# Mask rows in the score stacks, six slots, and scores issued ahead of values, in a windowed-attention block kernel

## What is computed

```python
q = (x @ Wq + bq).reshape(B, S, H, hd).transpose(0, 2, 1, 3)   # k and v alike, H = 16, hd = 8
scores = jnp.einsum('bhqd,bhkd->bhqk', q, k) * scale
allowed = (j <= i) & (i - j < WINDOW)                          # WINDOW = 32
scores = jnp.where(allowed, scores, NEG_INF)
attn = jax.nn.softmax(scores, axis=-1)
out = jnp.einsum('bhqk,bhkd->bhqd', attn, v)
out = out.transpose(0, 2, 1, 3).reshape(B, S, D)
return out @ Wo + bo
```

## Time and profile before

| | us |
|---|---|
| median of 3 runs | 146.55 (146.3 to 146.96) |
| profiled execution | 145.36 |
| its span, first to last instruction | 143.6 |
| TensorE busy | 110.2 (77%) |
| VectorE busy | 96.1 (67%) |
| ACT busy | 68.9 (48%) |
| GpSimd busy | 46.2 (32%) |
| transfer queue q1 | 20.26 MB, 49.4% of 16 engines |

### The profile page before, as it was taken

The page is one execution under the profiler, slowest core; times in us unless marked ns, Lnnn a source line. Parts: engine busy times, 40 slices in busy tenths (PEclk is TensorE's granted clock), DMA queues, the critical chain, the costliest instruction groups (busy, mean ns, idle before and its releaser), DMA issues.

```text
span 143.6 us, 6819 instructions
## 1 busy us (share of the span) xinstructions
PE 110.2 (77%) x2888; PEld 78.5 (55%) x2888; DVE 96.1 (67%) x254; ACT 68.9 (48%) x157; POOL 46.2 (32%) x67
## 2 busy tenths in 40 slices
PE   0368619579846959966868768587699999999992
PEld 0235505357634746844646546475455649595891
DVE  1571508998697979967969979999999551111031
ACT  3125604556466357445738639438724772433300
POOL 3473360739424006006005103602900299200000
PEclk9999986857999996899999999999999999999999
DMA  1699693946697866596655595491000000202022
GB/s 40 172 324 275 183 333 110 302 120 184 158 262 199 242 183 181 142 286 195 202 175 155 167 293 141 109 258 36 0 5 0 5 2 0 79 1 69 4 73 73
DMA packets 39734, 20.60 MB, mean 143 GB/s; under 512 B 1431, under 2 KB 39582, under 8 KB 39710
## 3 DMA queue, kind: packets, MB, share of 16 engines
q1 hardware_dynamic: 39710, 20.26, 49.4%
HBM read 10.82 MB, written 9.44 MB: 141 GB/s over the span
## 4 chain that ended last, share of the span: by engine, by line
PE 37%; DMA 21%; DVE 18%; issue 10%; SPq 5%; ACT 4%; DVEq 1%; POOL 1%; ACTq 0%
DMA KS<-k_scr 14%; PE bank_o L466 6%; DVE probsT L774 5%; PE bank_qk L584 5%; PE bank_s L489 5%; PE bank_v L584 4%; PE bank_o L489 4%; DMA k_scr<-k_parts 3%; SPq L227 3%; DVE negmax L759 3%; DVE centred L766 2%; DMA q_scr<-q_parts 2%; PE bank_s L443 2%; PE bank_w L512 2%; SPq L210 2%
## 5 line engine op out<-in xcount | busy, mean ns | idle before, releaser
L466 PE MATMUL bank_o<-V,probsT 128*32 128x36 f32 x1024 | 24.9, 206 | 13.1 <-DVE probsT L774 12.4
L654 ACT ACTIVATE probs<-centred 128x512 f32<-128x512 f32 x32 | 20.2, 631 | 26.2 <-DVE probsT L774 17.3
L466 PEld LDWEIGHTS bank_o<-V,probsT 128*32 128x32 f32 x1024 | 21.3, 118 | 18.3 <-issue 13.7
L759 DVE TENSOR_REDUCE negmax<-bank_s 128x8 f32<-128x512 f32 x32 | 21.6, 676 | 8.2 <-PE bank_s L443 8.2
L774 DVE STREAM_TRANSPOSE probsT<-probs 128x512 f32<-128x512 f32 x32 | 22.4, 699 | 0.0
L766 DVE TENSOR_TENSOR centred<-bank_s,negmax 128x512 f32<-128x512 f32 x32 | 21.2, 663 | 0.2
L269 POOL TENSOR_TENSOR q_parts<-rest,q_parts 128x256 bf16<-128x256 f32 x8 | 5.4, 672 | 43.2 <-ACT q_parts L601 43.2
L443 PEld LDWEIGHTS bank_s<-KS,QS 64*32 64x32 bf16 x1024 | 10.3, 98 | 13.2 <-issue 13.2
L436 PE MATMUL bank_s<-masks,ident_bf 128*128 128x512 bf16 x31 | 13.1, 423 | 3.9 <-DMA KS<-k_scr 2.4
L443 PE MATMUL bank_s<-KS,QS 64*32 64x64 bf16 x1024 | 14.6, 199 | 1.6 <-issue 1.6
L601 ACT ACTIVATE V<-bank_v 32x256 f32<-32x256 f32 x32 | 11.9, 371 | 0.4
(11 more groups left out here) (98 smaller groups left out, 200.3 us busy)
## 6 DMA issues: line engine op xcount, KB each, us to landing
QS<-q_scr SPq DMA_DIRECT2D x8, 512.0 KB, 4.2
KS<-k_scr SPq DMA_DIRECT2D x7, 576.0 KB, 5.9
q_scr<-q_parts SPq DMA_DIRECT2D x16, 192.0 KB, 3.0
k_scr<-k_parts SPq DMA_DIRECT2D x16, 192.0 KB, 3.1
q_scr<-q_parts SPq DMA_DIRECT2D x8, 128.0 KB, 3.0
k_scr<-k_parts SPq DMA_DIRECT2D x8, 128.0 KB, 2.2
x_sb<-in_L_attn_x_dram SPq DMA_DIRECT2D x1, 768.0 KB, 5.6
out_dram<-y SPq DMA_DIRECT2D x3, 256.0 KB, 2.3
```

The costliest lines, as they stand in the source:

```text
L466: mm = nc.tensor.matmul(o[q * WIN:(q + 1) * WIN, g * VC:(g + 1) * VC], probsT[s % 2][:, i, g, w, :], V[b][:, j + w, g, :], start=(w == 0), ...
L654: nc.scalar.activation(probs[s % 2][:], centred[s % 2][:].rearrange("p a k -> p (a k)"), ACT.Exp, scale=float(HD) ** -0.5).then_inc(probs_ ...
L759: nc.vector.tensor_reduce(negmax[s % 2][:], bank_s[s % 2][:].rearrange("p (a k) -> p a k", k=2 * WIN), AX.X, ALU.max, negate=True).then_in ...
```

## The change

- The mask is no longer a product of its own. A head's stack has 6 slots x 8 = 48 rows in one half of the 128 partitions; the other half holds an identity (in `QS`) and the mask (`bands`, in `KS`). Even and odd heads use opposite halves, so `QS` and `KS` get a further axis of 2. One score product goes over all 128 rows and adds the mask by the identity rows. The identity product of each unit goes.
- Two of the eight combinations of parts go: the high part is written to 3 slots, the middle part to 2, the low part to 1.
- The stacks are read by four transfers of 48 partitions instead of two of 128.
- VectorE fills the constant rows ahead of the loop (`fill_q`, `fill_k`) and once in step 2 (`fill_pad`). SyncE waits for them ahead of the first reads.
- The masks are made before the first variance root on GpSimd and spread first of all on TensorE.
- On TensorE scores of unit s+1 stand first in a step, ahead of values; `turn_x` moves from u = 1 to u = 0 and `project` from u = 2 to u = 1, and ACT's copies with them. On VectorE the transpose of unit s-2 stands first in a step.
- The clearing of `V[0]` and `V[1]` on GpSimd moves behind the low parts of chunks 0 and 1.

The diff, cut to its core:

```diff
-SLOTS = 8
-Q_PARTS = (range(0, 3), range(3, 6), range(6, 8))
-K_PARTS = (range(0, 8, 3), range(1, 8, 3), range(2, 8, 3))
+SLOTS = 6
+ROWS = HD * SLOTS
+Q_PARTS = (range(0, 3), range(3, 5), range(5, 6))
+K_PARTS = (range(1, 6, 2), range(2, 6, 2), range(0, 1))
...
-        QS = two("QS", [P, 2 * NG, CHUNK], BF16)
-        KS = two("KS", [P, 2 * NG, KW], BF16)
+        QS = two("QS", [P, 2, 2 * NG, CHUNK], BF16)
+        KS = two("KS", [P, 2, 2 * NG, KW], BF16)
...
                 if c >= 2:
                     sp.wait_ge(s_ps, UNITS * (c - 1))
+                else:
+                    sp.wait_ge(filled, 2 * c + 1)
                 sp.wait_ge(q_in[b], WRITES * (c // 2 + 1))
-                sp.dma_start(QS[b][:], q_scr[:, :, cols].rearrange("(n r) c t -> (r c) n t", n=2 * NG)
-                             ).then_inc(stacked[b], 16)
+                for odd in range(2):
+                    rows = slice(2 * WIN * odd, 2 * WIN * odd + ROWS)
+                    sp.dma_start(QS[b][rows, odd], q_scr[:, :, cols].rearrange(
+                        "(n e r) c t -> e (r c) n t", n=2 * NG, e=2)[odd]).then_inc(stacked[b], 16)
...
             ln1_rstd(2, TILES, 2 * TILES)
-            for b in range(2):
-                nc.gpsimd.memset(V[b][:, :, :, 0:GH * HD], 0.0).then_inc(v_set, 1)
             low_parts(0, 0)
+            nc.gpsimd.memset(V[0][:, :, :, 0:GH * HD], 0.0).then_inc(v_set, 1)
...
-                    nc.tensor.matmul(dst[:].rearrange("p (a k) -> p a k", k=2 * WIN), ident_bf[:],
-                                     masks[:, 0:1].to_broadcast([P, UB * NG, 2 * WIN]), start=True, stop=False)
...
-                                dst[hh * WIN:(hh + 1) * WIN, (i * NG + g) * 2 * WIN:(i * NG + g + 1) * 2 * WIN],
-                                QS[b][rows, n, j * WIN:(j + 1) * WIN], KS[b][rows, n, j * WIN:(j + 2) * WIN],
-                                start=False, stop=(i == UB - 1 and g == NG - 1))
+                                bank_s[s % 2][hh * WIN:(hh + 1) * WIN, (i * NG + g) * 2 * WIN:(i * NG + g + 1) * 2 * WIN],
+                                QS[b][:, hh % 2, 2 * g + hh // 2, j * WIN:(j + 1) * WIN],
+                                KS[b][:, hh % 2, 2 * g + hh // 2, j * WIN:(j + 2) * WIN], start=True, stop=True)
...
+                if s + 1 < SU:
+                    scores(turn, s + 1)
+                elif s + 1 == SU and not last:
+                    scores(turn + 1, 0)
                 if not (first and s < 3) and s < SU + 3:
                     values(turn if s >= 3 else turn - 1, (s - 3) % SU)
...
+                    if p1 and u == 0:
+                        turn_x(c + 2, b)
                     if p1 and u == 1:
-                        turn_x(c + 2, b)
-                    if p1 and u == 2:
                         project(c + 2, b)
...
+            def fill_q(b):
+
+                for odd in range(2):
+                    f = nc.vector.tensor_copy(QS[b][:, odd].rearrange("p n (m c) -> p (n m) c", c=2 * WIN),
+                                              ident_bf[:, 2 * WIN * (1 - odd):2 * WIN * (2 - odd)].unsqueeze(1).to_broadcast(
+                                                  [P, NG * BLOCKS, 2 * WIN]))
+                f.then_inc(filled, 1)
...
+            def fill_k(b):
+
+                for odd in range(2):
+                    f = nc.vector.tensor_copy(
+                        KS[b][:, odd, :, WIN:].rearrange("p n (m y k) -> p n m y k", y=2, k=WIN)[:, :, :, 1],
+                        bands[:, odd, 0:WIN].unsqueeze(1).unsqueeze(1).to_broadcast([P, 2 * NG, BLOCKS // 2, WIN]))
+                    f = nc.vector.tensor_copy(
+                        KS[b][:, odd, :, WIN:].rearrange("p n (m y k) -> p n m y k", y=2, k=WIN)[:, :, :, 0],
+                        bands[:, odd, WIN:].unsqueeze(1).unsqueeze(1).to_broadcast([P, 2 * NG, BLOCKS // 2, WIN]))
+                if b == 0:
+                    nc.vector.memset(KS[b][2 * WIN:, 0, :, 0:WIN], NEG)
+                    nc.vector.memset(KS[b][0:2 * WIN, 0, :, 0:WIN], 0.0)
+                    nc.vector.memset(KS[b][0:2 * WIN, 1, :, 0:WIN], NEG)
+                    f = nc.vector.memset(KS[b][2 * WIN:, 1, :, 0:WIN], 0.0)
...
+            dve.wait_ge(consts, 2)
+            fill_q(0)
             dve.wait_ge(x_first, 16)
             ln1_var(0, TILES)
...
             ln1_norm(0, 0)
+            dve.wait_ge(masks_set, 1)
+            fill_k(0)
             dve.wait_ge(x_second, 16)
             ln1_var(TILES, 2 * TILES)
...
+            fill_q(1)
+            fill_k(1)
             split_rest(1, 1)
...
+                if not (first and s < 2) and s < SU + 2:
+                    turn_probs(turn if s >= 2 else turn - 1, (s - 2) % SU)
                 if rows:
                     dve.wait_ge(x1_done, tile + 1)
...
-                if not (first and s < 2) and s < SU + 2:
-                    turn_probs(turn if s >= 2 else turn - 1, (s - 2) % SU)
+                if first and s == 2:
+                    fill_pad(0).then_inc(filled, 1)
```

More of the change, by code:

```diff
@@ L169, in block_kernel @@
         N_FIRST, N_W = 7, 6
-        STACKS = 2 * 16
+        STACKS = 4 * 16
         WRITES = PARTS * 16
@@ L299, in _ @@
-            for first in range(2):
-                nc.gpsimd.affine_select(out=tri[:, first], in_=tri[:, first], compare_op=ALU.is_ge, fill=NEG, base=WIN,
-                                        pattern=[[-1, 2 * WIN]], channel_multiplier=1).then_inc(consts, 1)
+            for row in range(2):
+                for own in range(2):
+                    at = tri[:, row, (1 - own) ^ row:6:4]
+                    nc.gpsimd.affine_select(out=at, in_=at, compare_op=ALU.is_ge if own else ALU.is_gt, fill=NEG, base=0,
+                                            pattern=[[0, 2], [-1 if own else 1, WIN]],
+                                            channel_multiplier=1 if own else -1).then_inc(consts, 1)
@@ L413, in project_v, with spread_bands @@
                 mm.then_inc(v_ps, 1)
[L415 removed]
+            def spread_bands():
                 pe.wait_ge(consts, 6)
[L418 to L420 removed]
+                for quad in range(GH):
+                    e = quad % 2
+                    row, first = (0 if e else 1), (2 if quad < 2 else 0)
+                    mm = nc.tensor.matmul(bank_w[quad * WIN:(quad + 1) * WIN, 0:4 * WIN], ident[0:WIN, 0:WIN],
+                                          tri[:, row, first:first + 4].rearrange("p n k -> p (n k)"), start=True, stop=True)
                 mm.then_inc(masks_ps, 1)
```

63 lines of the change are left out of this document (24 added, 39 removed).

## The result

The change makes the kernel slower: 150.41 us median (149.61 to 150.77, 4 runs) where before has 146.75 (146.3 to 147.8, 4 runs) beside it, a ratio of 1.023 with an interval of 1.016 to 1.030. The interval leaves open whether it is over 2%. The forecast was 139.7, its range ended at 145.0. The profiled execution has a span of 148.7 us; by the forecast it was to be 143.6 − 6.8 = 136.8.

What follows compares the result with a forecast made beforehand. VectorE was taken to bound the loop, TensorE the tail. First unit +1.0, loop waits −7.6, `fill_pad(0)` +0.2 and tail −0.4 sum to −6.8 us: 139.7 us against a median of 146.55, range 136.5 to 145.

Steps and rivals of the forecast that it cites:

- Identity product, 128-row scores: TensorE, each unit: dropping the product gains nothing in the loop, 0.5 us before the first unit; scores take 0.35 us.
- `turn_x` and `project` earlier: Loop: high parts ready about a step (2 us) before the residual split, removing VectorE's 6.0 us of waits.
- Slack 0.4 us at full clock: VectorE's residual add in odd steps: 0.4 us slack, 1.3 us charged for half clock and leftovers, 7.6 of 8.9 gained.
- Available are ... 13.4 − 0.5 = 12.9: Loop: 12.9 us available from split to stack landing against 12.5 needed, so 2.5 us of score waits go.
- The stack load, 6.4 us: New reads of 48 partitions: 6.4 us taken, between 5.2 at full rate and 8.2 at half; no gain.
- Rival (c): Stack reads at half rate: 8.2 us per load, chunks wait, first unit 1.8 us later; 144 us, chance 0.12.
- The fills: VectorE before the loop: `fill_q` 1.4 us, `fill_k(0)` 2.8; with the identity saving, first unit +1.0 us.
- Rival (a): Fills slow or blocked: at 1.0 ns per element the first unit is 5 us late; 143.7 us, chance 0.14.
- Rival (b), the clock: TensorE idles more, clock falls to half: +2.5 us per chunk, 149.7 us at four chunks; chance 0.09.
- Rival (d), waits that only move: Loop: `split_rest` waits for something else, half of the 7.6 us stays; 143.5 us, chance 0.08.
- Idle time of TensorE: Loop of the original kernel: TensorE idle 3 to 5 us per turn, so its saved work gains nothing there.
- The tail: TensorE's last stretch: two identity products (0.6 us) fall out, part still waits on `weff_done`; −0.4 us.

Runs made afterwards that it cites:

- turns_first: Original kernel with VectorE's weight transposes moved to the head of its step, nothing else: 144.47 us against 148.25, first series.
- early_project: Original kernel with only the transposes of x, the q and k projection and their copies one step earlier: 147.17 us, ratio 0.986 from 3 of 11 executions.
- early_turns: Original kernel with the projection one step earlier and VectorE's weight transposes first in the step, scores still behind values: 144.66 us, ratio 0.985.
- after_values_first: Changed kernel with scores put back behind values, output product and projection on TensorE: 147.51 us, ratio 1.003 to the original.
- fill_late: Changed kernel with VectorE's fills of stack 1 moved behind the rest of chunk 1 and the variances of tiles 4 to 7: 146.17 us, ratio 0.998 to the original.
- order_only: Original kernel with only the new order (scores first, transposes first, projection a step earlier): 148.63 us, ratio 1.015.
- boundary_late: Changed kernel with stack 1's fills later and scores behind values at chunk starts alone: 145.04 us, ratio 0.983 to the original.
- combo: Changed kernel with stack 1's fills later and scores behind values, output product and projection in every step: 145.72 us, ratio 0.989 to the original.
- slots_only: Original kernel with only six slots and stack reads of 48 partitions, order and identity product kept: 148.42 us, ratio 1.016.
- turns_first_again: Second series of the original kernel with only VectorE's weight transposes first in the step: 144.99 us, ratio 0.988.
- stacks_turns_first: Changed kernel with stack 1's fills later, transposes first on VectorE, projection and scores at their old places: 146.57 us against 147.52, no ratio.

## Why the prediction was wrong, point by point

- **Identity product, 128-row scores.** Held: 32 products in 0.35 us at full clock (at 41.80), and no gain in the loop.
- **`turn_x` and `project` earlier, "so the 6.0 us go".** The wait went, to 0.4 us; the time did not. The step charged the move as if nothing stood behind that wait. turns_first gives 1.2% without it, early_project nothing that is sure, and both together (early_turns) no more than turns_first.
- **"Slack 0.4 us at full clock ... I charge 1.3 us for this and other leftovers, so that 7.6 of 8.9 us are gained."** This is the step that failed. VectorE idles for 10.8 us in the loop, not 1.3, and the terms of −7.6 and +0.2 came out at +2.9 together (87.78 against 84.93). The prediction named the queue ("what is queued behind the scores' wait") and priced only the half clock in it. What the runs show in its place is 6.7 us of waits for the output projection and 2.3 for the values. 8.0 of these 9.0 us follow stalls of TensorE without a semaphore, which had no term in the sum, and 0.5 a wait for a stack. In the turn without stalls the forecast holds and more, 19.04 us for 19.3 to 19.8. Putting the scores back behind values and output projection gives 3.0 us (after_values_first) but takes only 1.5 to 2.5 of the 10.3 missing in the loop; the cause of the rest is tied to the stalls by their place in the traces, no run takes them away.
- **"Available are ... 13.4 − 0.5 = 12.9."** Wrong as well, by 2.1 us. A stack is wanted 2.6 us ahead of the row maximum when output projection and residual are queued behind it, so 10.8 are available. The chain from split to scores measured 89.91 − 79.16 = 10.75 us, better than the 12.5 forecast, and was just in time. This error costs 0.5 us here, 1.9 in fill_late's third turn and 5.2 in order_only.
- **The stack load, 6.4 us.** From the issue of the first Q read to the scores that wait for it, it takes 7.0 us (82.94 to 89.91) and 7.3 (94.50 to 101.84), with the packets at half rate and a quarter fewer bytes; before needs 7.6 (35.83 to 43.41), 7.8 and 6.6. So 6.4 was too low for both kernels by this measure, and "no gain" held. The Trainium skill's figure in the prediction, 7.2, is met in size, but the rise over before that it implied is not there. Rival (c) was right in its rate and wrong in its price and place: no load of the changed kernel that scores waited for took 8.2 us, and the first unit is not late by it (fill_late).
- **The fills.** Their price held: `fill_q` took 1.3 us (forecast 1.4), `fill_k(0)` 2.4 (forecast 2.8; from 5.64 to 8.08). The Trainium skill's figure in the prediction, 693 ns for 2,048 elements, is the price that the sum took (0.3 × 2,048 + 70 = 684 ns), so it was not near the lower bound, and the "+0.3" worked out from it should have been the sum's own +1.0. What they block was not asked: `fill_q(1)` and `fill_k(1)` stood in no term at all, and cost 3.1 us of the first unit (25.16 against 22.05 in fill_late; all other terms of +1.0 come out at −0.2). The prediction had seen VectorE's op of 2.12 us beside GpSimd's memset and moved that memset away; the lock goes the other way as well.
- **Rival (a)** named the place, "slow or blocked", but its price was for slow copies. Blocked was GpSimd, and the first unit is late by it as (a) would have it, 2.9 us.
- **Rival (b), the clock.** Not shown as a cause of its own. The clock was 0.80 and 0.83 in turns 1 and 3, low behind stalls in the one and behind waits of 1.44 and 1.04 us for VectorE in the other. It draws the waits out: at half clock values take 1.18 us in place of 0.71. But in their profiled executions boundary_late has a mean of 0.86 and combo 0.90 where before has 0.95, and both are faster than before.
- **Rival (d), waits that only move,** had 0.08 and is nearest to what happened. Its price, half of 7.6, was too low since it had no room for waits that are longer than those they replace.
- **Idle time of TensorE.** "3 to 5 us per turn" should read 4.1 to 5.4; nothing hangs on it.
- **The tail:** −0.7 us for a forecast of −0.4.

In sum, by the ratios, each by one edit from different kernels: the place of the fills costs 3.7 us (fill_late) and the scores ahead of values 3.0 (after_values_first), both together 5.1 (combo); the stacks' form costs 1.6% as far as slots_only shows (0.2 to 2.9%); the transposes first give 1.8 us (turns_first_again). What is left of the gain of 7.6 that was forecast is this last one.

## What to carry to other kernels

Before moving work ahead on an in-order engine, list what it waits for, and give that wait a deadline by what is then queued behind it, not by its own consumer. Removing one wait of the bounding engine is worth the distance to the next one: find that in a turn where all else is on time, and then ask how late the queue may be in the other turns. A sum that holds in the best turn leaves no room for what comes late in the rest. Put bulk copies of VectorE where GpSimd has nothing on the path, and keep a transfer in one piece over 128 partitions unless the bytes saved pay for the half rate.

## What the runs showed of the hardware that was not expected

- TensorE stands without a semaphore for 0.2 to 3.8 us at a time in turns during which four to six blocks of 16 KB are transferred on the instruction queue, up to 14.2 us in a loop of 86 us (stacks_turns_first), and in no profiled execution for more than 0.3 us at a time in the loop's second pass, with at most one such transfer. 96 instructions ahead of the loop move the places.
- A GpSimd operation of 0.67 us took 2.79 beside VectorE's copies of constant rows; in fill_late such a copy of 0.42 us took up to 1.35 beside GpSimd.
- A packet of 576 bytes takes 29 ns in transfers to 128 partitions, 49 in transfers to 64 and 58 in transfers to 48.
